# The last 42 hidden rows of the down projection in one matmul per tile, with their second copy made by DMA

## What is computed

```python
xn = layernorm(x)
q, k, v = split(xn @ Wqkv + bqkv)                 # 256 -> 3 x 256
qp, kp = elu(q) + 1, elu(k) + 1
kv, k_sum = kp.T @ v, kp.sum(tokens)              # one per sequence
z = layernorm(xn + (qp @ kv) / (qp @ k_sum + 1e-6)) * g1 + b1
h = silu(z @ Wg + bg) * (z @ Wu + bu)             # 256 -> 682
s = layernorm(z + h @ Wd + bd) * g2 + b2          # 682 -> 256, the down projection
out = x + s * silu(xn @ ternary(weight).T)
```

## Time and profile before

| | |
|---|---|
| median of 3 runs | 1328.03 us (1326.86 to 1335.59) |
| span of the profiled execution | 1331.0 us |
| PE busy | 97% of the span |
| DVE busy | 87% |
| ACT busy | 71% |
| POOL busy | 48% |
| time in which DMA packets of q1 run, share of 16 engines | 12.9% |

### The profile page before, as it was taken

The page is one execution under the profiler, slowest core; times in us unless marked ns, Lnnn a source line. Parts: engine busy times, 40 slices in busy tenths (PEclk is TensorE's granted clock), DMA queues, the critical chain, the costliest instruction groups (busy, mean ns, idle before and its releaser), DMA issues.

```text
span 1331.0 us, 25237 instructions
## 1 busy us (share of the span) xinstructions
PE 1285.1 (97%) x8147; PEld 1152.5 (87%) x8147; DVE 1159.3 (87%) x2900; ACT 940.7 (71%) x1626; POOL 632.6 (48%) x683
## 2 busy tenths in 40 slices
PE   7889999999999999999999999999999999999995
PEld 5779898898898989889888888888989888988884
DVE  6987888989888988988989888989888988878886
ACT  5697777777777877677777677777677777756641
POOL 4732444554534554544554544554543554533343
PEclk8999999999999999999999999999999999999998
DMA  6200011111011111011111011111001111111100
GB/s 195 80 17 17 1 49 49 49 48 49 9 41 48 49 49 49 6 43 49 49 49 48 17 33 49 49 49 49 23 27 49 49 32 33 33 33 33 33 16 32
DMA packets 57895, 55.81 MB, mean 42 GB/s; under 512 B 5967, under 2 KB 56997, under 8 KB 57766
## 3 DMA queue, kind: packets, MB, share of 16 engines
q1 hardware_dynamic: 57766, 54.20, 12.9%
HBM read 37.41 MB, written 16.78 MB: 41 GB/s over the span
## 4 chain that ended last, share of the span: by engine, by line
PE 76%; DVE 16%; issue 4%; ACT 2%; POOL 1%; DMA 0%; SPq 0%; DVEq 0%; ACTq 0%; POOLq 0%
PE bank L917 57%; PE d_bank L917 14%; DVE rz L803 5%; DVE rz L798 4%; PE xk_bank L917 3%; DVE hs L767 3%; DVE h_l L777 2%; PE bank L931 2%; ACT h_h L476 1%; DMA bk1b<-in_L_attn_bqkv_dram 0%; DVE xn L682 0%; DVE kp L709 0%; POOL rz L318 0%; DVE kp_l L715 0%; POOL rz L320 0%
## 5 line engine op out<-in xcount | busy, mean ns | idle before, releaser
L424 POOL TENSOR_TENSOR rstd<-ve,neg_half 128x4 f32<-128x4 f32 x96 | 100.7, 1049 | 506.1 <-DVE ve L667 506.1
L917 PE MATMUL bank<-zT_h,wgu_h 128*128 128x512 f32 x704 | 280.7, 399 | 0.2 <-DVE zT_l L755 0.2
L917 PE MATMUL bank<-zT_l,wgu_h 128*128 128x512 f32 x704 | 278.7, 396 | 0.0
L917 PE MATMUL bank<-zT_h,wgu_l 128*128 128x512 f32 x704 | 278.7, 396 | 0.0
L476 ACT ACTIVATE hs<-bank,hb 128x512 f32<-128x512 f32 x192 | 131.5, 685 | 116.0 <-DVE h_l L777 79.9
L777 DVE TENSOR_TENSOR h_l<-hs,h_h 128x512 fp32r<-128x512 f32 x160 | 150.6, 944 | 61.9 <-ACT h_h L476 60.7
L917 PE MATMUL d_bank<-wd_h,h_h 128*128 128x256 f32 x640 | 183.7, 287 | 12.5 <-DVE h_l L777 12.5
L318 POOL TENSOR_TENSOR rz<-rz,sg 128x256 f32<-128x256 f32 x126 | 124.8, 990 | 145.9 <-DVE rz L803 145.9
L917 PE MATMUL d_bank<-wd_l,h_h 128*128 128x256 f32 x640 | 180.8, 283 | 0.0
L917 PE MATMUL d_bank<-wd_h,h_l 128*128 128x256 f32 x640 | 180.4, 282 | 0.0
L917 PEld LDWEIGHTS bank<-zT_l,wgu_h 128*128 128x128 f32 x704 | 132.4, 188 | 31.3
(11 more groups left out here) (125 smaller groups left out, 3553.6 us busy)
## 6 DMA issues: line engine op xcount, KB each, us to landing
xa<-in_L_attn_x_dram SPq DMA_DIRECT2D x32, 512.0 KB, 5.7
xq<-in_L_attn_x_dram SPq DMA_DIRECT2D x32, 512.0 KB, 4.9
out_dram<-rz SPq DMA_DIRECT2D x31, 512.0 KB, 3.4
rz<-in_L_attn_Wg_dram SPq DMA_DIRECT2D x1, 640.0 KB, 4.4
rz<-in_L_attn_Wu_dram SPq DMA_DIRECT2D x1, 640.0 KB, 5.4
sg<-in_L_attn_Wd_dram SPq DMA_DIRECT2D x1, 640.0 KB
qp<-in_L_attn_Wqkv_dram SPq DMA_DIRECT2D x1, 512.0 KB, 4.7
out_dram<-rz SPq DMA_DIRECT2D x2, 256.0 KB, 2.1
```

The costliest lines, as they stand in the source:

```text
L424: eng.tensor_tensor(dst, ve[:, k, :], neg_half[:, 0:1].to_broadcast([P, TILES]), ALU.pow).then_inc(S[f"rs{k}"], 1)
L917: ins = eng.matmul(dst, left, right, start=first and n == 0, stop=last and n == len(pairs) - 1, **kw)
```

## The change

D 5 gets one matmul per tile. `ht` keeps the high part in rows 0 to 41 and the low part in rows 64 to 105; a second copy of the high part goes to rows 42 to 63 (its rows 0 to 21) and 106 to 125 (its rows 22 to 41). `wd_h` gets the low weights at the same rows, copied once from `wd_l`. Both biases are added into one row (126, its low part in 127). The copy of the activations is two DMAs for each group, issued by SP at the end of its iteration (`again_rows`) once `hh` says that ScalarE has written them; D 5 waits for both through the new semaphore `s_again`. The copy of the weights is three DMAs issued once by SP in iteration -1, after `setup_d_tail`.

```diff
@@ SP
+            def again_rows(g):
+
+                eng.wait_ge(S["hh"], HC * (g + 1))
+                for to, of, n in ((HT, 0, SPLIT), (UT + HT, SPLIT, HT - SPLIT)):
+                    eng.dma_start(ht[to:to + n, :].bitcast(f32), ht[of:of + n, :].bitcast(f32))\
+                       .then_inc(s_again, 16)
...
                     (iteration -1, behind the hb1 loads)
+                    eng.wait_ge(S["w_dt"], 1)
+                    for to, of, n in ((HT, 0, SPLIT), (UT + HT, SPLIT, HT - SPLIT), (BIAS + 1, BIAS, 1)):
+                        eng.dma_start(wd_h[to:to + n, HF, :].bitcast(f32), wd_l[of:of + n, HF, :].bitcast(f32))\
+                           .then_inc(s_wdt, 16)
                 if a + 2 < GROUPS:
                     load_xa(a + 2)
...
                 if 3 <= q + 1 < GROUPS:
                     load_xq(q + 1)
+                if 0 <= i < GROUPS:
+                    again_rows(i)
@@ DVE
+            def setup_d_bias():
+
+                eng.wait_ge(s_w["d"], 16 * 5)
+                eng.tensor_tensor(raw_d[:, HF, :], raw_d[:, HF, :], raw_d[:, HC, :], ALU.add)\
+                   .then_inc(S["w_db"], 1)
+
             def setup_d_tail():
                 eng.wait_ge(S["w_dh"], 1)
-                eng.memset(wd_l[UT:P, HF, :].bitcast(f32), 0.0).then_inc(S["w_dt"], 1)
-                eng.tensor_tensor(wd_l[0:UT, HF, :], raw_d[0:UT, HF, :], wd_h[0:UT, HF, :].bitcast(f32),
+                eng.tensor_tensor(wd_l[:, HF, :], raw_d[:, HF, :], wd_h[:, HF, :].bitcast(f32),
                                   ALU.subtract).then_inc(S["w_dt"], 1)
@@ PE, in Dn
-                        eng.wait_ge(S["w_dt"], 2)
+                if c == HF:
+                    eng.wait_ge(s_again, 16 * 2 * (g + 1))
+                    if g == 0:
+                        eng.wait_ge(s_wdt, 16 * 3)
...
-                        pairs = ((ht[:, s], wd_h[:, c, :]), (ht[:, s], wd_l[:, c, :]))
+                        pairs = ((ht[:, s], wd_h[:, c, :]),)
```

More of the change, by code:

```diff
@@ L38 @@
 UT = 64
+SPLIT = UT - HT
+BIAS = P - 2
 BATCH, SEQ = 8, 2048
@@ L101 @@
 FILL_VECTOR = steps("""
-    a_stats 0, k_add 0, k_add 1, k_add 2, k_max 0, setup_gu_low_0 2, setup_ternary 3, setup_bq 2,
+    a_stats 0, k_add 0, k_add 1, k_add 2, k_max 0, setup_d_bias 1, setup_gu_low_0 2, setup_ternary 3, setup_bq 2,
     k_add 3, k_low 0, k_max 1, a_norm 0, k_max 2, k_max 3, k_low 1, k_low 2, xT_low 0, k_low 3,
@@ L249, in build_kernel @@
         s_cst = sem("s_cst")
+        s_wdt = sem("s_wdt")
+        s_again = sem("s_again")
         names = ("warm w_bq1 w_bk w_qkh w_qkl w_abs w_sum w_scale w_half "
-                 "w_neg w_tern w_ternT w_tern_r w_b1w w_row w_hb w_guh w_gul w_dh w_dl w_dt "
+                 "w_neg w_tern w_ternT w_tern_r w_b1w w_row w_hb w_guh w_gul w_db w_dh w_dl w_dt "
                  "bn0 ag0 ve0 rs0 xn nm0 xh xl TX xTh xTl K k1 mK eK kp kph kpl ks XK xk KV kv kvh kvl "
@@ L360, in _ @@
                 eng.dma_start(raw_d[at:at + HT, HF, :], wd[HF * P:H, :]).then_inc(s_w["d"], 16)
-            eng.dma_start(raw_d[HT:HT + 1, HF, :], row(bd)).then_inc(s_w["d"], 16)
-            eng.dma_start(raw_d[HT + 1:HT + 2, HF, :], row(b1)).then_inc(s_w["d"], 16)
+            eng.dma_start(raw_d[BIAS:BIAS + 1, HF, :], row(bd)).then_inc(s_w["d"], 16)
+            eng.dma_start(raw_d[BIAS:BIAS + 1, HC, :], row(b1)).then_inc(s_w["d"], 16)
             eng.dma_start(wv[:, :, :], rows(wqkv[:, 2 * D:3 * D])).then_inc(s_w["v"], 16)
@@ L403, in _ @@
             eng.memset(raw_tail, 0.0).then_inc(s_clear, 1)
-            eng.memset(raw_d[:, HF, :], 0.0).then_inc(s_clear, 1)
+            eng.memset(raw_d[:, HF:HC + 1, :], 0.0).then_inc(s_clear, 1)
             eng.memset(ident[:, :], 0.0).then_inc(s_cst, 1)
@@ L624, in setup_d_high @@
             def setup_d_high():
-                eng.wait_ge(s_w["d"], 16 * 5)
+                eng.wait_ge(S["w_db"], 1)
                 act(wd_h[:, :, :], raw_d[:, 0:HC, :], ACT.Copy, "w_dh")
@@ L896, in _ @@
                 run_steps(FILL_VECTOR if filling(i) else VECTOR_STEPS, {
-                    "setup_q_low": (a, lambda: setup_qk_low(0)), "setup_bq": (a, setup_bq),
+                    "setup_d_bias": (a, setup_d_bias), "setup_q_low": (a, lambda: setup_qk_low(0)), "setup_bq": (a, setup_bq),
                     "setup_gu_low_0": (a, lambda: setup_gu_low(0)), "setup_gu_low_1": (a, lambda: setup_gu_low(1)),
```

## The result

The changed kernel takes 1462.68 us (median of 4 runs, 1459.65 to 1466.32) against 1327.44 us before: **1.102 times the time before, 95% interval 1.098 to 1.105**. It is slower by 135 us; 1417 us had been forecast, in a range up to 1455.

What follows compares the result with a forecast made beforehand. TensorE (PE), busy 1285 of 1331.0 us, was taken to bound the kernel. 1331.0 - 15.2 (matmuls) + 81.8 (waits) + 20 (clock) + 2.5 (opening) = 1420 us span, so a 1417 us median; range 1362 to 1455.

Steps and rivals of the forecast that it cites:

- What is removed: D 5 on TensorE: four matmuls dropped in each of 32 groups, 128 x 0.119 = 15.2 us less.
- The landing: Activation copies queued behind store and xq load: landing 5.55 us after the store's issue, 5.6 with the matmul restart.
- The sum of the waits: Stalls of D 5 for the copies, summed over groups by their store-to-D 5 distances: 81.8 us, bounds 28 and 108.
- That it is paid in full: Main loop: no work hides D 5's stall and each group pays again, so nothing is taken off the 81.8 us.
- The clock: TensorE's clock falls after stalls of 3.2 us or more: 20 us lost, between 0 and 30.
- The price for one stall: TensorE after a long D 5 stall: 1.6 us lost to the 1.2 GHz clock level.
- Two in three: Share of the 19 D 5 stalls of 3.2 us or more taken to lower TensorE's clock, giving 20 us.
- a rival named it: TensorE's clock falls after every stall, or for twice as long: 1427 to 1460 us; full or longer loss or later landing 0.15.
- The opening: Iteration -1: weight copies ahead of load_xa(6) make DVE late by 5 us; 2.5 us cost, bounds 0 and 5.
- The rival of overtaking copies: Copies don't queue behind the 1 MB: stall 28 to 49 us, 1344 to 1365 us; overtaking or partly hidden 0.15.
- The bound from below: D 5's copies: three 0.44 us issues, then the smallest store's 2.1 us; landing 3.4 us after the store, 28 us stall.
- The other side: D 5's wait is hidden and four matmuls are gained: 1313 us, 1315 with the opening; chance 0.03.

Runs made afterwards that it cites:

- the other order in the opening: Changed kernel with the three weight copies moved in iteration -1 behind the load of xa for group 6: 1445.35 us, 1.0824 of the kernel before.
- the second experiment: Changed kernel with the activation copies issued behind the same wait for the last result, but ahead of the store and xq load: 1348.63 us, 1.0115 of the kernel before.
- the filled wait: Changed kernel with 13 unused matmuls (5 in groups with KV) ahead of D 5 in groups 1 to 25: 1421.11 us, 1.0653 of the kernel before.
- no copies: Kernel before with the second matmul of each tile in D 5 left out and no copies added: 1321.22 us, 0.9899 of the kernel before.
- both moves: Changed kernel with activation copies ahead of store and xq load, weight copies behind the xa load for group 6: 1324.87 us, 0.9927 of the kernel before.

## Why the prediction went wrong, and where it was right

The direction and the place were right, and so was the mechanism but for how often the clock falls and how long it stays down; the time, 1463 us, lies above the range. By its own steps:

- **What is removed**, 15.2 us: 13.3 us measured alone, with 15.3 as the interval's end. Right.
- **The landing**, 5.55 us after the store's issue and 5.6 to D 5: 5.68 and 5.82 in the iteration shown (710.63 and 710.77 against 704.95). The copies land 0.44 us behind xq where 0.3 was reckoned. But the iteration shown is one of the quicker ones: over groups 1 to 29 D 5 starts 6.06 us behind the store's issue on average, 5.96 in the second trace. That is 0.4 us in each of 29 groups.
- **The sum of the waits**, 81.8 us: 85.1 in one trace, 96.7 in the other. The forecast used the distances of the earlier trace rows, with 2 groups at 0.7 us. They are no property of a group: in the first trace of the changed kernel D 5 of 5 groups fell due 0.9 us behind the store, in the second that of none. The five are worth 8.5 us (1.7 each), and the range had no term for it.
- **That it is paid in full**, because VectorE and the results move with TensorE: right. VectorE's step behind D 5 waits 3.42 us where it waited 0.24, and D 5 falls due 2.56 us behind the store's issue in the usual group, where it was 2.4.
- **The clock**, 20 us out of bounds 0 to 30: 44 us, 37 in the second trace. This is the step that failed. The price for one stall, 1.6 us, came out at 1.7 for the usual one. "Two in three" did not: of the waits of 2.5 us and more all 21 had a low stretch in the first trace and all but one in the second, and so had some shorter ones. Six stretches were twice as long, which the earlier trace rows did not show and the bounds left out (a rival named it, 1427 to 1460 us), though the trace held an instance of it: from 10.8 to 17.7 us the kernel before ran at 0.50 (a stretch of it stands below), from 1.3 us behind an idle of 2.5 us and with one of 1.3 us inside. The Trainium skill (TensorE: Matmul & The Clock Gate, "HAM oscillation") would have had every pass of the loop pay; the traces agree with that for 40 of 41 waits of 2.5 us and more in the changed kernel and for 17 of 20 with the other order in the opening, and not for the passes whose wait was under 1.7 us. It had been given the weight of a rival where it was the likelier case.

```profile
11.00:17.50 6.50, 5.46 (x25) 5.50 (x26) 4.56 (x15) 3.50 (x10) 3.52 (x4) 0.50 0.91 253
```

- **The opening**, 2.5 us out of 0 to 5: the load cost 4.9 and 4.7 us in the two traces, at the upper bound, and the opening as a whole 7. VectorE was 7.1 us late at its first step, where 5 was reckoned: the three issues took 2.26 us instead of 1.4, and the subtraction ahead of them ended 0.8 us later. The 1.75 us did go off: VectorE's step for `qp` comes 5.2 us late (97.04 against 91.86). PE lost 3.5 us of these in idle, where 2.5 was taken, and 1.3 by the clock behind it, for which this step had no term.
- **The rival of overtaking copies**: excluded by the traces, since they came behind xq. The bound from below that it used holds: with an empty queue (the second experiment) the copies land 2.10 us after the second issue begins, the time of the smallest store.
- **The other side** (the wait is hidden) is excluded for this order, and is what happened once the two lines stood 5 us earlier, 0.4% under the time before, or 0.7% with the weight copies moved as well.

Together 15 us too little in waits (in the first trace), 24 in clock and 4.5 in the opening make 43.5 us; 41.5 lie between the 1420 forecast for the span and the 1461.5 of the trace. The median was missed by 46, since it stands 1 us above this span where it had stood 3 below the one of before.

## What to carry to other kernels

Before a small DMA is put on the path of the busiest engine, read what stands ahead of it in the issuer's list and in its queue, at the place where it goes: here its data were ready 5 us before they were wanted, and a foreign wait (2.6 us), two issues (1.0), a megabyte ahead (1.8) and the copies themselves (3.05) used up 8.5. Where an idle of some us is put into each pass of a loop that keeps TensorE full, count its clock too, here for every pass that waits 2.5 us or more and not for some; it added 44 us to 97. A table of distances taken from one trace is a sample of how engines happened to fall, and a range should hold the other case.

## What was not expected of the hardware

Two VectorE operations and one GpSimd addition that run at the same time come out in one of two ways. The rows are the same instructions in two iterations of the changed kernel.

```profile
650.16 0.88 DVE L815 SCALAR_TENSOR_TENSOR rz<-rz,mv,g2b 128x256 f32<-128x256 f32 x2
650.27 2.76 POOL L324 TENSOR_TENSOR rz<-rz,xq 128x256 f32<-128x256 f32 x1
...
695.39 1.36 DVE L815 SCALAR_TENSOR_TENSOR rz<-rz,mv,g2b 128x256 f32<-128x256 f32 x2
695.50 0.97 POOL L324 TENSOR_TENSOR rz<-rz,xq 128x256 f32<-128x256 f32 x1
```

Either VectorE is slowed (1.36 us for the pair instead of 0.88) or GpSimd is held up (2.76 us instead of 0.97). The second makes the store 1.7 us later against TensorE: these are the groups with 0.7 us between store and D 5 in the kernel before, 0.9 in the changed one. The kernel before had two of them (additions of 2.77 us from 277.01 and 435.51), the changed kernel 5 in one trace and none in the other, the kernel with the copies at the store 10, that with the other order in the opening 7, that with the copies ahead 17, those with the filled wait, with no copies and with both moves none; each of the five in the changed kernel is followed by one of its five waits of 5.0 us or more. Where D 5 does not wait, the same event makes the iteration shorter: 38.55 us from D 5 to D 5 against 39.28 in the kernel before. The kernel with the copies ahead takes 974.9 us from D 5 of group 1 to that of group 26, that with both moves, which has no such event, 982.1. This is the likely reason why the traced run of the former was 7.4 us under its median; the other runs have no trace. What decides between the two ways was not tried; that they run at the same time is read from the rows, and a shared path to the memory would explain it but was not tested apart.
